# Norms of an attention and expert kernel moved to VectorE, weight halves shared out anew, routing and loads reordered

## The reference

```python
x = x + attention(layernorm(x), ctx)      # softmax(q k^T / 16) v, one head of 256
h = layernorm(x)                          # 2048 tokens of 256
probs = softmax(h @ Wr.T)                 # 8 experts; the best two, weights divided by their sum
for e in range(8):                        # W1[e] is 1024 x 256, W2[e] is 256 x 1024
    y = gelu(h @ W1[e].T + b1[e]) @ W2[e].T + b2[e]
    out += y * w_e[..., None]             # w_e: weight of expert e, 0 where it isn't chosen
x = x + out
```

## Time and profile before

| what | us |
|---|---|
| median of three runs | 424.75 (424.51 to 425.94) |
| the profiled execution, its own time | 427.02 |
| its span in the trace | 425.2 |
| TensorE busy | 344.2 |
| GpSimd busy | 288.5 |
| ScalarE busy | 236.5 |
| VectorE busy | 233.5 |

### The profile page before, as it was taken

One profiled execution on the slowest core, in us unless ns is written; L12 is line 12 of the kernel. 1 busy time (PEld: TensorE's weight loads), 2 busy tenths in 40 slices (PEclk: granted clock), 3 DMA queues, 4 the chain that ended last, 5 costly groups with the idle time before them and its releaser, 6 DMA issues.

```text
span 425.2 us, 10292 instructions
## 1 busy us (share of the span) xinstructions
PE 344.2 (81%) x3412; PEld 292.6 (69%) x3412; DVE 233.5 (55%) x539; ACT 236.5 (56%) x491; POOL 288.5 (68%) x272
## 2 busy tenths in 40 slices
PE   8894959659865674389399989999999999999940
PEld 7463636544654353288398879999999999999940
DVE  3077716762667398834648745555555555555530
ACT  2675655636473434146455656666666666666620
POOL 5759683768898898565828777666667556755741
PEclk9996999679988996869889999999999999999995
DMA  8996363426350202353242334434334355433321
GB/s 272 374 274 212 90 229 100 136 99 199 123 164 25 74 0 75 109 117 90 51 39 77 65 56 61 63 53 54 52 52 64 41 51 53 64 43 51 39 28 23
DMA packets 51602, 40.85 MB, mean 96 GB/s; under 512 B 29248, under 2 KB 47296, under 8 KB 51424
## 3 DMA queue, kind: packets, MB, share of 16 engines
q1 hardware_dynamic: 41024, 26.97, 24.2%
q0 software_dynamic: 7584, 10.57, 14.9%
q10 hardware_dynamic: 2944, 2.66, 1.9%
HBM read 22.40 MB, written 12.66 MB: 82 GB/s over the span
## 4 chain that ended last, share of the span: by engine, by line
DMA 37%; POOL 35%; issue 20%; PE 3%; POOLq 1%; ACT 1%; DVE 0%; ACTq 0%
DMA out<-y,meta 36%; POOL rows L477 10%; POOL w1h L463 9%; POOL w2h L427 8%; POOL rstd L422 3%; POOL send L470 2%; DMA wk_sb<-WkT 1%; POOL v_sb L427 1%; PE s_ps L629 1%; PE proj L616 1%; PE proj L595 1%; POOL out L518 1%; POOL gates L537 1%; POOL gates L534 1%; POOL gates L531 1%
## 5 line engine op out<-in xcount | busy, mean ns | idle before, releaser
L518 POOL DMA_INDIRECT out<-y,meta x39 | 66.9, 1717 | 61.2 <-DMA out<-y,meta 55.0
L1382 DVE TENSOR_SCALAR gh<-g,up 128x512 f16<-128x512 f32 x78 | 40.6, 521 | 95.2 <-ACT g L1011 95.2
L1011 ACT ACTIVATE g<-s_ps,b_sb,down 128x128 f32<-128x128 f32 x156 | 62.8, 453 | 51.7 <-PE s_ps L760 51.6
L777 PE MATMUL o_ps<-w2h,gh 128*128 x312 | 85.5, 274 | 1.8 <-DVE gl L1384 0.8
L777 PE MATMUL o_ps<-w2l,gh 128*128 x312 | 85.5, 274 | 0.0
L777 PE MATMUL o_ps<-w2h,gl 128*128 x312 | 85.5, 274 | 0.0
L1011 ACT ACTIVATE g<-t_ps,b_sb,down 128x128 f32<-128x128 f32 x156 | 62.6, 453 | 29.3 <-PE t_ps L760 25.2
L760 PE MATMUL s_ps<-xs,w1h 128*128 128x128 f16 x624 | 61.4, 222 | 10.7 <-DMA xs<-rows 10.7
L760 PE MATMUL t_ps<-xs,w1h 128*128 128x128 f16 x624 | 62.0, 223 | 0.0
L1384 DVE SCALAR_TENSOR_TENSOR gl<-g,up,gh 128x512 f16<-128x512 f32 x78 | 58.6, 752 | 2.8
L477 POOL DMA_INDIRECT rows<-send,place x32 | 44.6, 1393 | 22.1 <-DVE place L1196 13.4
(11 more groups left out here) (194 smaller groups left out, 613.5 us busy)
## 6 DMA issues: line engine op xcount, KB each, us to landing
staged<-W1T SPq DMA_DIRECT2D x5, 1024.0 KB, 5.7
staged<-W2T SPq DMA_DIRECT2D x4, 1024.0 KB, 7.2
x_sb<-x SPq DMA_DIRECT2D x4, 512.0 KB, 4.4
w1l<-W1T SPq DMA_DIRECT2D x2, 1024.0 KB, 11.4
w2l<-W2T SPq DMA_DIRECT2D x2, 1024.0 KB, 11.8
out<-x_sb ACTq DMA_DIRECT2D x4, 512.0 KB, 4.9
rows<-send POOLq DMA_DIRECT2D x8, 130.0 KB, 6.3
ctx_sb<-ctxT SPq DMA_DIRECT2D x4, 256.0 KB, 5.8
```

Source lines behind the costliest of these rows:

```text
L518: pool.indirect_dma_start(out=out, out_offset=bass.IndirectOffsetOnAxis(ap=meta[:, t % XR, 3:4].bitcast(I32), axis=0), in_=y2[:, t % YR, : ...
L777: i = nc.tensor.matmul(y_ps[t % 2][:, 0:D], l[:, t % 2, m, :], second_weight(w, m, e), start=(m == 0 and k == 0), stop=(m == MC - 1 and k ...
L1011: i = nc.scalar.activation(g[:, t % 2, m, :], h_ps[s][:, (m % MQ) * TR:(m % MQ + 1) * TR], ACT.Gelu, bias=b1_sb[:, bass.ds(e, 1), m:m + 1] ...
L1382: nc.vector.tensor_scalar(gh[:, u, m, :], g[:, u, m, :], by, None, ALU.mult).then_inc(g_high, 1)
```

## The change

- The application of both norms moves from GpSimd to VectorE (`ln1_apply`, `ln2_apply`); the inverse root stays on GpSimd.
- The high halves of units 12 and 14 move from GpSimd to ScalarE (`HIGH_ON_SCALAR`).
- On VectorE the low half of the odd unit of a pair now mostly comes before the even one. Stages and the order of the loads follow.
- In the attention loop `ranks(b − 1)` moves behind the next batch's queries, `route_places` to the start of the batch after, `early_tables` behind the second residual of batch 3. On ScalarE `rows_hi` follows the last `square` of a batch.
- In the expert stage `ranks(2)` moves to (1, 2), `ranks(3)` to (4, 2), the gates of batch 3 to t = 3, its places to t = 4 and the late tables to t = 4, 5 and 6.
- The first choice's exponential is taken as 1 (`first_exp` goes).
- The transfer of `b2` waits for 14 low halves, not 16, and `b2_sb` has another place.

```diff
-STAGE_OF = (0, 1, 2, 3, 4, 5, 0, 1, 4, 2, 3, 5, 0, 4, 1, 2)
+STAGE_OF = (0, 1, 2, 3, 4, 5, 0, 1, 2, 4, 3, 5, 1, 4, 0, 2)
-LOW_ORDER = (0, 1, 2, 3, 4, 5, 6, 7, 8, 9, 10, 11, 13, 12, 14, 15)
+LOW_ORDER = (1, 0, 3, 2, 4, 5, 7, 6, 8, 9, 11, 10, 13, 12, 15, 14)
+HIGH_ON_SCALAR = (1, 3, 5, 7, 9, 11, 13, 12, 15, 14)
...
-            load_unit(6)
             load_unit(7)
             load_ctx(1)
+            load_unit(6)
+            load_unit(10)
+            load_unit(8)
+            load_x(2)
             load_unit(9)
-            load_unit(10)
-            load_x(2)
-            load_unit(8)
             load_unit(11)
...
+            load_unit(15)
             load_unit(13)
-            load_unit(15)
...
-            first_normal(0)
+            rsqrt(0, 0, ln_var, ln_rstd)
...
             high(0)
-            first_normal(1)
+            rsqrt(0, 1, ln_var, ln_rstd)
             high(2)
-            second_normal(0)
+            rsqrt(1, 0, ln2_var, ln2_rstd)
             split_low(0)
             high(4)
-            first_normal(2)
+            rsqrt(0, 2, ln_var, ln_rstd)
             high(6)
-            second_normal(1)
+            rsqrt(1, 1, ln2_var, ln2_rstd)
             split_low(1)
             high(8)
             send_rows(0, 0)
-            first_normal(3)
+            rsqrt(0, 3, ln_var, ln_rstd)
             high(10)
+            rsqrt(1, 2, ln2_var, ln2_rstd)
             send_rows(0, 1)
-            second_normal(2)
             split_low(2)
-            high(12)
-            high(14)
             send_rows(1, 0)
             send_rows(1, 1)
-            second_normal(3)
+            rsqrt(1, 3, ln2_var, ln2_rstd)
...
                 if not last:
-                    if b:
-                        ranks(b - 1)
                     values(b + 1)
                     queries(b + 1)
                     add_all(b, "end")
+                    if b:
+                        ranks(b - 1)
...
-                if (t, m) == (0, 7):
+                if (t, m) == (1, 2):
                     ranks(B - 2)
...
-                if (t, m) == (3, 4):
+                if (t, m) == (4, 2):
                     ranks(B - 1)
...
             softmax_half(3)
             high(13)
+            high(12)
             logits_half(3)
             high(15)
             soft(3, 3)
             take_turned(3, 2)
+            high(14)
             take_turned(3, 3)
...
                 row_max(b, 0)
                 row_max(b, 1)
+                if b >= 2:
+                    route_places(b - 2)
                 low(u)
                 row_max(b, 2)
                 invert(b, 0)
+                low(u + 1)
                 route_logits(b - 1)
-                low(u + 1)
+                ln1_moments(b + 1)
                 residual(b, 0)
-                ln1_moments(b + 1)
                 row_max(b, 3)
                 invert(b, 1)
-                route_first(b - 1)
+                ln1_apply(b + 1)
                 residual(b, 1)
                 scale(b, "middle")
+                route_first(b - 1)
                 route_second(b - 1)
                 invert(b, 2)
                 invert(b, 3)
                 residual(b, 2)
-                low(u + 2)
                 residual(b, 3)
                 aggregate(1, b, stats2_ready, ln2_var)
-                route_places(b - 1)
                 low(u + 3)
+                ln2_apply(b)
                 route_gates(b - 1)
+                low(u + 2)
                 scale(b, "end")
...
             scale(b, "begin")
-            early_tables()
+            route_places(b - 2)
             row_max(b, 2)
             invert(b, 0)
+            low(13)
             route_logits(b - 1)
-            low(13)
             residual(b, 0)
             row_max(b, 3)
             invert(b, 1)
             low(12)
             residual(b, 1)
+            early_tables()
             invert(b, 2)
             invert(b, 3)
-            low(14)
             residual(b, 2)
             low(15)
             residual(b, 3)
             aggregate(1, b, stats2_ready, ln2_var)
+            low(14)
...
                 if t == 2:
                     route_first(B - 1)
                     route_second(B - 1)
+                if t == 3:
                     route_gates(B - 1)
-                if t == 3:
+                if t == 4:
                     route_places(B - 1)
-                if t == 4:
                     late_tables_1()
+                if t == 5:
                     late_tables_2()
-                if t == 5:
+                if t == 6:
                     late_tables_3()
```

More of the change, by code:

```diff
@@ L85, in projection_order @@
             order += steps("xt", b + 1, DC)
+            order += steps("v", b + 1, VW) + steps("q", b + 1, DC) + sums(b, "end")
             if b:
                 order += steps("rank", b - 1, 1)
-            order += steps("v", b + 1, VW) + steps("q", b + 1, DC) + sums(b, "end")
     order += steps("rank", B - 2, 1)
@@ L950, in _ @@
             queries(1)
+            square(6)
             rows_hi(0)
-            square(6)
             softmax_half(1)
@@ L969, in _ @@
             queries(2)
+            square(11)
             rows_hi(1)
-            square(11)
             softmax_half(2)
@@ L1306, in _ @@
             ln1_moments(b + 1)
-            low(0)
+            low(1)
             residual(b, 0)
@@ L1316, in _ @@
             residual(b, 2)
-            low(2)
             residual(b, 3)
@@ L1320, in _ @@
             low(3)
+            ln2_apply(b)
+            low(2)
             scale(b, "end")
             for b in range(1, B - 1):
-                u = 4 if b == 1 else 8
+                u = 4 * b
                 row_max(b, 0)
                 row_max(b, 1)
+                if b >= 2:
+                    route_places(b - 2)
                 low(u)
```

87 lines of the change are left out of this document (45 added, 42 removed).

## The result

The changed kernel takes 399.81 us (median; 398.55 to 400.7), the kernel before beside it 425.21. The ratio is 0.94, 95% interval 0.9363 to 0.9438. The profiled execution took 400.7 us with a span of 399.0, where the kernel before had 427.02 and 425.2: 26.2 us less span.

What follows compares the result with a forecast made beforehand. Two halves were taken: attention bound by a chain of waits, experts by TensorE, meeting at the first tile. Gains 3.6 + 7.3 − 2.7 + 3.0 + 6.4 + 0.9 = 18.5 gave 406.3, said as 407 us; range 400 to 417.

Steps and rivals of the forecast that it cites:

- Term F: Expert stage: late routing one tile later saves 6.6 us of wait and half clock, loses 5.3 and 0.4; 0.9 gained.
- D: Start of batch 3: sends and copy of rows let soft(3,0) start at 136.7 instead of 147.93; 3.0 us net gained.
- A + B + C: Up to batch 2's first maxima: norms 3.6, ranks and places behind queries 7.3, VectorE late −2.7; net 8.2 us earlier.
- Term A: First softmax after batch 1 starts: norms on VectorE let high(4) start earlier; 3.6 us gained.
- Term B: Between batch 1's attends and batch 2's scores: ranks and places behind the queries remove TensorE's wait in values; 7.3 us gained.
- Term E: Batch 3 to tile 0: high halves 12 and 14 on ScalarE, tables after the maxima; 6.4 us gained, tile 0 near 165.
- The first: Rival: GpSimd's high halves hold VectorE to their end, norms included; gain only 9.8, 415 us; 16%.
- The second rival: Expert stage: VectorE reaches the late routing's places a whole tile later, delaying adds; 5.3 us more, 412 us; 12%.
- The third, alternation: Batches 1 and 2: VectorE and GpSimd alternate instead of overlapping, 5.4 us a turn; all eight give 450 us; 5%.
- the fourth: Batches 2 and 3: sends before inverse root or rows_hi each meet a low half; 15 us more, 422 us; 5%.

Runs made afterwards that it cites:

- e1: Changed kernel with both norms applied on GpSimd again; 414.39 us, ratio 0.9608 to the kernel before.
- e15: Changed kernel with batch 3's late gates, places and tables a tile earlier and early tables before its third maximum; 397.68 us, ratio 0.9229.
- e6: Kernel before with only the norms moved to VectorE, all orders as before; 415.10 us, ratio 0.9772.
- e3: Changed kernel with ranks before the values again and, on VectorE, places and gates behind the aggregate; 405.97 us, ratio 0.9433.
- e4: Changed kernel with high halves 12 and 14 on GpSimd again, ahead of the sends of batch 1; 414.08 us, ratio 0.9624.
- e10: Changed kernel with the early tables put before the third row maximum of batch 3; 406.72 us, ratio 0.9446.
- e18: Kernel before with norms on VectorE, low halves behind them and batch 3 as changed; an edit slip left the engines idle, and it ended after 2.86 us.
- e9: Changed kernel with the sends of batch 0's second choice put before high(10) on GpSimd; 409.02 us, ratio 0.9486.
- e7: Changed kernel with VectorE's late places and tables of batch 3 one tile earlier; 396.16 us, ratio 0.9321.

## Why the prediction was wrong in size

**Direction and mechanism held.** The first tile is the meeting point, and the expert stage stayed at TensorE's pace. These came as said: four norm calls in 1.36 us (1.0 to 2.1; 1.2 taken); first maxima of batch 2 at 93.92 (94.3); soft(3,0) released by the copy of rows; last wait before tile 0 for a low half; 1.04 us at ranks(3) (1.7), 6.4 at (7,4) (5 to 6), tile 9 63.0 us after tile 0 (62.8). Term F was 0.9 and came out as 1.0, closer than the spread of such stages allows to claim. The marks for scores(3,0), soft(3,0) and tile 0 were missed, all on the early side: 123.39, 132.95 and 159.9 for 127, 137 and 165. Neither condition for "wrong" was met: tile 0 was before 172, and tile 0 to the end is 239.1, 2.6 off 241.7. Neither would have caught a tile 0 that comes early.

**The step that failed is the size of the walk from the first maxima of batch 2 to tile 0 (Terms D and E).** In the prediction's own terms, as the profiles have them:

| term | forecast | measured |
|---|---|---|
| A + B + C, at the first maxima of batch 2 | 8.2 | 8.6 |
| D, from there to soft(3,0) | 3.0 | 6.4 |
| E, from there to tile 0 | 6.4 | 7.7 |
| F, the expert stage | 0.9 | 1.0 |
| the tail, no term | 0 | 2.5 |

At the first maxima of batch 2 the forecast was 0.4 us late. At the fourth (107.89 against about 109.5) it is 1.6, at the scores of batch 3 (123.39 against 126.8) 3.4, at soft(3,0) (132.95 against 136.7) 3.75, at tile 0 (159.9 against 165) 5.1. So errors of 1.2 and 1.8 us came in batch 2, where I had said that it "repeats batch 1" and shifted rows of before by batch 1's gain and by 7.3; a shift keeps every stall of the old order that the new one lacks. Of the 1.2 two such stalls can be seen: high(8) started 1.04 us after the first maximum before and 0.19 after it now (94.11), and an idle stretch of 0.86 us of VectorE for the logits (before 112.88) is gone. Of the 1.8, some 0.9 is in the prediction's own sum: 8.7 and 7.3 are 16, and it took about 15. Batch 2's measured gain is 6.3 us as a stage, mine was 15 − 10.9 = 4.1.

For soft(3,0) the walk had the inverse root of batch 2 end at 126.0, and it ended at 123.70. The four sends took 0.3 less than priced. For their landing I took the median, 2.7; the last send landed within 1.6 of its issue's end. These are 2.3, 0.3 and 1.1 of the 3.75. Behind soft(3,0) the walk was 1.35 too long: 1.8 us too long up to the end of the fourth maximum of batch 3, 0.3 too long from there to the end of low(14), and 0.75 too short for the start of TensorE behind it. That took 1.95 us, where the prediction had 1.2, and no row of before shows it.

**The tail** had no term. The last add is issued 5.4 us after the last product, before it was 7.9 (417.11 and 409.20). That is the 2.5 us. The adds follow each other 4.7 to 4.9 us apart at the end of both kernels. In the profile of before the add of tile 36 starts 3.4 us behind its rows' last operation on ScalarE, here 0.8, so no queue is left. As said above, e1 and e15 have the long tail too, and it isn't shown that the change shortened it. With 5.1 and 2.5 in place, and 0.1 of Term F, 18.5 becomes 26.2 between the profiles. Between the medians (425.21 and 399.81) the gain is 25.4, and 1.7 is left for the tail and for chance. "Small unpriced port waits are all on one side", the reason for rounding up from 406.3 to 407, took the forecast 0.7 us further off: the unpriced items together were gains.

**Attribution was worse than the sum.** Term A overlaps with the new order (e1, e6), Term B's waits were real but TensorE's order didn't make them (e3), and Term E's parts have both signs: the high halves 7.5, the tables −3 to −4 (e4, e10). Parts undone one at a time (norms 5.2 to 7.6, high halves 7.5, ranks −1.4, low halves 1.0 to 2.3, tables −3 to −4) don't add to 22.7, and those put in one at a time (8.4, then 3.8) leave 10.5 that no run divides, since e18 gave nothing. It holds the high halves, the places, the ranks and the loads together. What the runs do show is how parts fail to add: at a meeting point the next chain stands close behind. For soft(3,0) the first maximum is ready near 130.1 and the copy of rows at 133, and an edit that shortens the one and lengthens the other (e9) gains nothing.

**Rivals.** The first priced the port waits to the end of the high half. Under high(6) and high(10) a two-input operation ended 3.76 and 3.75 us after GpSimd's began (76.26 + 3.51 − 76.01; 112.94 + 3.51 − 112.70), as priced at 3.8. By the rule of the Trainium skill's page "SBUF — State Buffer", in "SBUF: two separate sides", that whoever starts first has the shared pair for the whole instruction, it would be 5.4; the trace disagrees for this form, and agrees for the CAST at 98.25, which ends at 99.57 with its high half. The second rival didn't come, though the margin was thin: its wait of 6.4 at (7,4) is the one that e7 removes. The third, alternation, has no sign: of the four norms on VectorE in batches 1 and 2 none waits 1 us for its root. Of the fourth, three of the eight sends of batch 0 are stretched (3.06, 2.49 and 2.64), not all.

## What to carry to other kernels

Walk a changed order from its own first instruction; don't shift the stretches of the old trace, since they keep the old stalls, and here the error grew by 1.2 and 1.8 us within one batch. Before a cause is credited with what it is worth, undo it alone: here a change of order priced at 7.3 us a batch could be taken back at no cost, while the order of two loads was worth 8.3. And put it in alone too: the norms and the new order each brought the same high half forward, and a part undone in the presence of the other shows only what it has for itself. An order of compute that frees buffers is also an order of loads: look for the small urgent transfer that stands behind a blocked large one in the same queue.

## What the runs showed of the hardware

A low half on VectorE that begins first holds GpSimd's high half too: high(2), at 39.17, took 7.46 us, not 5.44, beside low(0), which ran from 38.98 to 41.33. A two-input operation of VectorE that meets a high half of 5.44 us was held until 3.7 to 3.8 us after the high half's start in every case looked at: 76.26, 95.41 and 112.94 in the changed kernel, 148.83 and 154.39 before, 114.64 in e9.

The kernel before took 424.6 to 425.2 us or 430.3 to 430.8, 1.3% more, at different times and on one chip both. The profiles of the second kind show 6 to 8 us more in tile 2 of the expert stage. A part of it stands in idle stretches of TensorE of up to about 1 us that the trace gives to nothing ("issue").
